# A mixture-of-experts kernel: the last four experts' weights are loaded behind the pads of the routed rows

## What is computed

```python
def _moe_forward(x, Wg, W1, W3, W2, Ws1, Ws3, Ws2):
    xt = x.reshape(-1, D)
    scores = jax.nn.softmax(xt @ Wg.T, axis=-1)
    sg = scores.reshape(T, G, E // G)
    group_scores = sg.max(axis=-1)
    gidx = jax.lax.top_k(group_scores, TOPK_G)[1]
    ...
    topi = jax.lax.top_k(masked, TOPK)[1]
    weights = jnp.take_along_axis(scores, topi, axis=1) * ROUTE_SCALE
    combine = jnp.zeros((T, E), xt.dtype).at[jnp.arange(T)[:, None], topi].add(weights)
    h = jax.nn.silu(jnp.einsum('td,eid->eti', xt, W1)) * jnp.einsum('td,eid->eti', xt, W3)
    expert_out = jnp.einsum('eti,edi->etd', h, W2)
    y = jnp.einsum('etd,te->td', expert_out, combine)
    z = jax.nn.silu(xt @ Ws1.T) * (xt @ Ws3.T) @ Ws2.T
    return (y + z).reshape(B, S, D)

x = x + _L0_xattn_ref(_layernorm(x, axis=-1), L0_xattn_k, fside_S2_0, ctx_2048, ctx_2048, 8)
x = x + _L0_ffn_ref(_layernorm(x, axis=-1), ...)
```

## Time and profile before

| | |
|---|---|
| median of 3 runs | 427.58 us (426.92 to 427.83) |
| the profiled execution's own time | 428.87 us |
| its span, first to last instruction | 427.1 us |
| granted TensorE clock, mean | 0.986 |
| busy: PE, DVE, ACT, POOL | 93%, 55%, 41%, 46% |
| DMA, mean over the span | 187 GB/s |

### The profile page before, as it was taken

One profiled execution on the slowest core, in us unless ns is written; L12 is line 12 of the kernel. 1 busy time (PEld: TensorE's weight loads), 2 busy tenths in 40 slices (PEclk: granted clock), 3 DMA queues, 4 the chain that ended last, 5 costly groups with the idle time before them and its releaser, 6 DMA issues.

```text
span 427.1 us, 9265 instructions
## 1 busy us (share of the span) xinstructions
PE 398.8 (93%) x2157; PEld 296.2 (69%) x2158; DVE 233.5 (55%) x596; ACT 176.9 (41%) x543; POOL 198.6 (46%) x247
## 2 busy tenths in 40 slices
PE   6999999989999997399889999999999999999993
PEld 5888888878787454165476777777777777777772
DVE  3575788888786535127723444444444434443973
ACT  5348466546443530101103433344343334446662
POOL 3253323357786657376201433343343334346874
PEclk9999999999999999879999999999999999999999
DMA  7964655648879967144332344433343444478678
GB/s 241 341 219 151 223 174 184 225 160 294 268 247 356 298 235 269 71 158 159 110 99 69 119 132 130 126 125 128 122 130 118 134 120 128 135 227 259 225 251 305
DMA packets 45914, 79.69 MB, mean 187 GB/s; under 512 B 6144, under 2 KB 35168, under 8 KB 43840
## 3 DMA queue, kind: packets, MB, share of 16 engines
q1 hardware_dynamic: 39024, 59.57, 43.5%
q0 software_dynamic: 6864, 19.80, 11.9%
HBM read 54.95 MB, written 24.40 MB: 186 GB/s over the span
## 4 chain that ended last, share of the span: by engine, by line
PE 83%; DVE 4%; another core or an unknown queue 4%; issue 3%; DMA 2%; POOLq 1%; POOL 1%; ACT 1%; SPq 0%; DVEq 0%
PE heads L1221 21%; PE bank L1278 15%; PE heads L1129 12%; PE heads L1256 8%; PE heads L1131 6%; PE bank L1268 5%; PE bank L1244 4%; PE heads L1231 4%; PE bank L1143 4%; DVE kv L694 2%; PE bank L1154 2%; DMA toep<-toep_in 2%; PE bank L1170 1%; POOLq L671 1%
## 5 line engine op out<-in xcount | busy, mean ns | idle before, releaser
L663 POOL DMA_INDIRECT y_scratch<-toep,dest_i x64 | 61.5, 960 | 119.1 <-DVE dest_i L1002 114.6
L1221 PE MATMUL heads<-w,toep 128*128 x316 | 106.8, 460 | 1.6 <-ACT toep L473 1.1
L1129 PE MATMUL heads<-toep,kv 128*128 128x256 f32 x256 | 77.9, 386 | 4.9 <-DVE kv L694 2.2
L1278 PE MATMUL bank<-w,toep 88*128 x316 | 81.2, 379 | 0.0
L605 POOL DMA_INDIRECT rows_scratch<-rows,slot_i x64 | 64.1, 1001 | 28.8 <-issue 19.6
L1221 PEld LDWEIGHTS heads<-w,toep 128*128 128x128 f32 x316 | 53.6, 190 | 19.1 <-issue 2.3
L479 ACT ACTIVATE toep<-heads 128x176 f32<-128x176 f32 x79 | 25.0, 317 | 78.0 <-PE heads L1221 73.2
L1278 PEld LDWEIGHTS bank<-w,toep 88*128 88x128 f32 x316 | 53.8, 190 | 4.7
L1131 PEld LDWEIGHTS heads<-toep,kv 128*128 128x128 f32 x256 | 48.6, 190 | 6.6
L723 DVE TENSOR_TENSOR prod<-heads,ctx_rep 128x1024 f32<-128x1024 f32 x32 | 39.0, 1220 | 24.6 <-PE bank L1143 20.8
L1131 PE MATMUL heads<-toep,kv 128*128 128x128 f32 x256 | 49.2, 274 | 0.0
(11 more groups left out here) (180 smaller groups left out, 490.6 us busy)
## 6 DMA issues: line engine op xcount, KB each, us to landing
ctx_rep<-ctxr_in SPq DMA_DIRECT2D x16, 1024.0 KB
toep<-rows_scratch SPq DMA_DIRECT2D x65, 144.0 KB
w<-w_in SPq DMA_DIRECT2D x16, 352.0 KB
w<-w_in SPq DMA_DIRECT2D x16, 176.0 KB
rows_scratch<-pad_row SPq DMA_DIRECT2D x17, 144.0 KB
ctx_tr<-ctxt_in SPq DMA_DIRECT2D x16, 128.0 KB
toep<-toep_in SPq DMA_DIRECT2D x4, 512.0 KB, 8.5
ctx_n<-ctx_in SPq DMA_DIRECT2D x16, 128.0 KB, 2.0
```

The source lines that it names most:

```text
L663: pool.indirect_dma_start(y_d, bass.IndirectOffsetOnAxis(ap=dest.bitcast(U32), axis=0), y_sb[b], None).then_inc(y_sent[b], 16)
L1129: nc.tensor.matmul(y_ps[par][:, i, :], kv[:, q, 0, h * P:(h + 1) * P], toep[:, q * HH + h, :], start=True, stop=False)
L1221: last = nc.tensor.matmul(up_ps[p], x_tr[p][:, blk, :], w13[:, bass.ds(e, 1), blk, :].rearrange("p a n -> p (a n)"), start=blk == 0, stop= ...
L1278: last = nc.tensor.matmul(dn_ps[p], hid_tr[p][:, c, :], w2[:, bass.ds(e, 1), c, :].rearrange("p a n -> p (a n)"), start=c == 0, stop=c == 1)
```

## The change

The loop over the last four experts, with its wait for `slots_ready`, moves from ahead of the pads to behind them. It then stands directly before the waits that precede the first gather. Nothing else is changed, and the other four engines have the same instructions in the same order.

```diff
             with sp.Fori(0, E - LATE) as e:
                 load_expert(e, w_in)
-            sp.wait_ge(slots_ready, BATCHES - 1)
-            with sp.Fori(E - LATE, E) as e:
-                load_expert(e, w_in)
 
             sp.wait_ge(pad_ready, 1)
             with sp.Fori(0, E) as e:
                 at = sp.value_load(pad_at[0:1, bass.ds(e, 1)], min_val=0, max_val=E * REGION)
                 sp.dma_start(rows_d[bass.ds(at, P)], pad_row[:, 0, :]).then_inc(padded, 16)
             sp.dma_start(rows_d[E * REGION:E * REGION + P], pad_row[:, 1, :]).then_inc(padded, 16)
+            sp.wait_ge(slots_ready, BATCHES - 1)
+            with sp.Fori(E - LATE, E) as e:
+                load_expert(e, w_in)
             sp.wait_ge(map_ready, 1)
```

## The result

The change costs time. Before took 427.58 us (median of 5 runs, 426.37 to 427.83), after 434.12 us (432.96 to 440.12, 5 runs): a ratio of 1.018, with a 95% interval of 1.014 to 1.022, or +6.5 us at the medians (+7.6 by the ratio). The forecast was 433.7 us.

A forecast was written before the change was run, and what follows sets the result against it. PE was taken to bound the kernel nearly everywhere, alone in the routed stage. A weight wait of 4.6 us plus 1.5 for the clock, with 0 for the stall's release, gave 427.58 + 6.1 = 433.7 us; range 429.2 to 436.8, widened to 425.5 to 437.

The forecast's parts named there:

- The direction and the place: End of shared stage: PE newly idles ahead of L1316 until the late weights land, delaying the routed stage; slower 0.82.
- The wait, 4.6 us: Ahead of L1316: PE arrives at 219.07 and goes on when the late weights land at 223.65, 4.6 us.
- The lower and upper end that I gave the data: Late weights' transfer behind the pads: 5.3 us at least, 2.3 us slower than the estimated 7.0 at most.
- The clock, 1.5 us: Behind PE's new idle time, partly on the first tiles: a stretch at granted clock 0.50 costs 1.5 us, ends 0 and 2.3.
- The release of the stall: Shared stage, PE's 18.34 us wait to 178.82: without weights there its end may come up to 1.3 us earlier; taken as 0.
- DVE's small delays of the earlier trace: Routing steps at 166.06 and 170.35: DVE lost 1.76 and 1.11 us, worth nothing since they lie under the stall.
- The first rival: Shared stage, 160 to 178.8 us: the late weights cause the stall and it goes; 424.9 us in all, chance 0.18.
- The third rival: Shared stage: the stall shrinks in part, released 3 us earlier, taking 3 of the 6.1 us; 430.7 us, chance 0.07.
- The second rival: First gather: held-up SP issues bring rows later than weights, first `turn_x` 6.0 us later; 435.1 us with clock, chance 0.11.

The follow-up runs named there:

- the first experiment: Changed kernel (after), with SP also waiting for all weights to land ahead of the first gather: 435.23 us, ratio 1.015 against before.
- the pair: After and before run again unchanged on the third chip, both profiled: after 436.54 us (ratio 1.019), before 428.28 (1.002), against 427.90 us.
- the fourth experiment: Before, with at most two of POOL's scatters in flight from unit 6 on: 431.06 us, ratio 1.008.
- That run: After, with the last four experts' weights on their own semaphore, awaited only after the first eight tiles: 435.06 us, ratio 1.016 against before.
- two kernels of before's time: On the second chip, before with four scatters in flight (413.55 us) and before with only experts 14 and 15 behind the pads (413.35), against 413.51.

## Why the prediction was right, and where its steps were off

**The direction and the place.** As forecast, SP's idle time had hidden the late weights and nothing hides them behind the pads; the new idle time stands ahead of L1316, is released by the transfer of the weights, and pushes the whole routed stage.

**The wait, 4.6 us, is the term that was mis-sized.** It was 7.5 us in after's profile, 7.8 in the first experiment and 8.4 in the pair. In the pair: the load takes 11.5 us from first issue (212.93) to release (224.41) in place of 8.6, +2.9; and PE gets there 3.06 us behind the first issue (215.99 - 212.93) in place of 4.02, +1.0; with the 4.6 that is 8.4. The +1.0 is no effect of the change: in before, L1316 follows the last pad's issue by 4.6 us in the earlier trace rows and by 3.4 in the pair's trace, so that distance varies by itself. The +2.9 comes from dividing in the wrong place. I took q1's share out of the elapsed time (62.1% of 11.3 us) and added an ideal start and end. Yet the earlier trace rows held the elapsed time itself: 155.93 to 168.2 is 12.3 us, and alone on the engines it is still 11.5 to 11.8. The scatters beside it had stretched it by little. The lower and upper end that I gave the data (5.3 and 9.3 us) held neither, since with the start and the signal they make 6.9 and 10.9. By the limit of about 358 GB/s that the Trainium skill gives ("DMA: Bandwidth & Descriptors", Specifications) the data would take an estimated 6.0 us; here they took 10.9 at a mean of 199 GB/s, so a limit is no forecast of the end of eight transfers where the wait is for the last one.

**The clock, 1.5 us.** It cost 1.44 us in the pair, as the pure price of 16 transposes at the 1.2 GHz level. But the size is not fixed: in the execution of 440.12 us the low stretch lasts 17 us and reaches the first tiles. Its span is 3.8 us longer than the pair's 434.5, of which 0.7 lies ahead of the first `up()` (229.23 against 228.55). After's other runs spread from 433 to 438 us, and the mean clock does not account for that: the run of 437.81 us had 0.977 and that of 434.12 had 0.978. What makes this spread is open.

**The release of the stall, taken at 0 with 1.3 as an end.** It was 1.1 us in the pair, inside that end; the other 0.7 us by which PE goes on earlier lie ahead of the change. DVE's small delays of the earlier trace rows, which I gave no worth, take late weights and scatters together: in the pair, DVE's wait at L829 (2.6 us in before) and PE's at L1182 (3.12) are gone in after, and in the fourth experiment, with the weights in their old place and two scatters in flight, they are gone as well. What stands behind them still ends under the stall.

**How two errors met.** 4.6 + 1.5 + 0 = 6.1 was forecast; 8.4 + 1.4 - 1.5 = 8.3 was measured in the pair, 8.6 at its medians and 6.5 at the medians of the first runs. The forecast's 433.7 us is thus nearer to the first result than its terms deserve, which is luck in part; against the third chip it is 2.5 us short. Why the change cost 6.5 us on one occasion and 8.6 on another is open; the intervals of the two ratios overlap.

**The first rival**, that the late weights cause the stall, falls: with no weights there, 16.6 to 17.5 us of ACT's wait remain, and a limit of two on the scatters alone takes it away. **The third rival**, part of the stall, holds for 1.1 of the 3 us that it assumed. **The second rival**, rows later than the weights, had the right mechanism and the wrong condition. I tied it to late issues, and misread their size: 163.16 is the eighth issue, whose regular place is 160.5 and not 159.9, so they were 2.7 us late, not 3.3. The issues were on time, and still the gather landed with the weights (5.46 us in place of at most 2.4). The Trainium skill ("DMA: Bandwidth & Descriptors", Queues, rings and completion order) states that each DMA engine consumes the descriptors of a queue in ring order. That run agrees; but a mere share of the engines would give the same landing, and no run here tells the two apart.

## What to carry to other kernels

Price a moved load by the time from its first issue to its last landing, as the trace has it, not by its share of the engines: the tail of the slowest engine is part of it. An engine's long wait is free cover for whatever stands behind it in its queue; before work is moved out of such a wait, look for the idle time that it will find in the new place, and count how much of it fits. On the second chip PE came 7.2 us behind the first late issue and half of the load fitted; on the third it came after 3.1 us, where the whole load took 11.5. Half of it was not tried there. Where one wait is taken away and little is won, look for a second one with the same end.

## What was not expected of the hardware

- **Held-back signals.** While POOL's scatters run without a pause, ACT stands up to 17.8 us before a step whose matmuls PE had finished 12.4 us before it went on; with two scatters in flight it stands 5.4, which is PE's own work. With four it was 28.9 us on one chip, and on the second chip 24 scatters without a pause held up nothing. What holds the signal back stays open.
- **The chip matters.** The same kernel took 413.5 us on one chip and 427.9 to 428.6 on two others, with a granted clock of 0.993 to 0.998 against 0.98 or so. By the traces the difference lies ahead of the routed stage: on the fast chip two kernels of before's time reach the 16 transposes at 202.8 and 203.3 us, without the stall, where before in the pair does at 217.5. Why that chip has no stall is open.
- **A load's tail.** Eight transfers, 2.16 MB, alone on the engines, took 11.8 us from first issue to release at 8.1 us of engine time; four of them (half the bytes) at most 7.2.
- **SP's pace.** The loop over the 16 pads took 26 us where nothing stalled, 31 to 32 with before's or after's stall, and 48.7 with the longest one, though SP waits for nothing in it.
